# Row sums from VectorE's output step, squared distances on ScalarE, and the choice of experts spread over VectorE's other work

## The reference

```python
x = x + attention(layernorm(x))     # linear attention with running sums over the tokens
x = x + experts(layernorm(x))       # 8 experts, each token goes to the one with the largest logit
x = x + time_mix(layernorm(x))
x = x + experts(layernorm(x))

def layernorm(x, eps=1e-5):
    m = mean(x); v = var(x)         # over the 128 values of a token
    return (x - m) / sqrt(v + eps)
```

## Time and profile before

| what | value |
|---|---|
| median of three runs | 301.19 us |
| the profiled execution | 301.99 us, of which the span that the trace covers is 300.3 us |
| PE, DVE, ACT, POOL busy in the span | 93%, 79%, 61%, 75% |
| attention, from the first `project_qk` to the last tile of it scattered in time for the experts' first stage | about 9 to 73 us |
| experts, first time | about 78 to 156 us |
| time mix | about 157 to 230 us |
| experts, second time | about 230 to 300 us |

### The profile page before, as it was taken

One profiled execution on the slowest core, in us unless ns is written; L12 is line 12 of the kernel. 1 busy time (PEld: TensorE's weight loads), 2 busy tenths in 40 slices (PEclk: granted clock), 3 DMA queues, 4 the chain that ended last, 5 costly groups with the idle time before them and its releaser, 6 DMA issues.

```text
span 300.3 us, 7709 instructions
## 1 busy us (share of the span) xinstructions
PE 278.1 (93%) x2179; PEld 242.9 (81%) x2179; DVE 238.6 (79%) x1018; ACT 183.3 (61%) x543; POOL 225.7 (75%) x296
## 2 busy tenths in 40 slices
PE   7989999986899999999999899999799799999994
PEld 7556676764599999999984688877599799999994
DVE  4888999999787887777753999888977499777773
ACT  2876666532489876666630774652399566666661
POOL 3868388887878888887562757888578888888654
PEclk9999999999999999999999999999999799999998
DMA  6898810001332554321105400111321455332100
GB/s 183 244 353 222 89 40 29 27 29 33 96 75 80 127 110 112 90 74 61 33 5 170 113 0 1 45 48 45 75 81 48 116 120 111 102 95 58 46 25 2
DMA packets 32521, 25.64 MB, mean 85 GB/s; under 512 B 6000, under 2 KB 28785, under 8 KB 32480
## 3 DMA queue, kind: packets, MB, share of 16 engines
q1 hardware_dynamic: 27328, 16.51, 23.2%
q0 software_dynamic: 4576, 8.54, 8.7%
q10 hardware_dynamic: 576, 0.10, 0.2%
HBM read 14.57 MB, written 11.53 MB: 87 GB/s over the span
## 4 chain that ended last, share of the span: by engine, by line
PE 52%; DVE 16%; POOL 16%; issue 7%; DMA 6%; SPq 1%; ACT 0%; DVEq 0%; POOLq 0%; ACTq 0%
PE pair L1648 20%; PE pair L1634 14%; POOL sorted L511 10%; PE bank L1634 5%; POOL rows L485 3%; DVE stats L826 3%; PE bank L1624 2%; DMA sorted<-rows,place 2%; DVE zT L1066 2%; DMA rows<-x_mid 1%; DMA xs<-sorted 1%; DVE mv L831 1%; PE pair L1473 1%; DVE qk L1059 1%; PE pair L1419 1%
## 5 line engine op out<-in xcount | busy, mean ns | idle before, releaser
L1648 PE MATMUL pair<-w2s,hT 128*128 x624 | 83.6, 278 | 0.6 <-issue 0.4
L511 POOL DMA_INDIRECT sorted<-rows,place x64 | 64.7, 1010 | 17.8 <-issue 15.3
L1648 PEld LDWEIGHTS pair<-w2s,hT 128*128 128x128 f32 x624 | 76.5, 194 | 1.0 <-issue 0.7
L1634 PE MATMUL pair<-xsT,w1s 128*128 128x128 f32 x432 | 60.3, 277 | 0.9 <-ACT xsT L765 0.9
L1634 PEld LDWEIGHTS pair<-xsT,w1s 128*128 128x128 f32 x432 | 54.4, 194 | 1.7 <-DVE tm L1134 1.0
L688 ACT COPY w1s<-w1all 128x516 f32 x78 | 49.4, 635 | 3.6 <-DVE etab L1208 2.5
L531 POOL DMA_INDIRECT out<-ys,xs x39 | 39.4, 1009 | 12.7 <-DVE ys L1280 7.3
L531 POOL DMA_INDIRECT x_mid<-ys,xs x39 | 39.4, 1010 | 12.4 <-DVE ys L1280 7.2
L765 ACT COPY xsT<-bank 128x128 f32<-128x128 f32 x78 | 20.8, 267 | 43.5 <-PE bank L1624 41.6
L1280 DVE SCALAR_TENSOR_TENSOR ys<-pair,xs 128x128 f32<-128x128 f32 x78 | 27.2, 349 | 24.4 <-PE pair L1648 24.3
L1270 DVE TENSOR_SCALAR hT<-pair,w1s 128x128 f32<-128x128 f32 x112 | 34.4, 346 | 1.3
(11 more groups left out here) (172 smaller groups left out, 522.5 us busy)
## 6 DMA issues: line engine op xcount, KB each, us to landing
xs<-sorted SPq DMA_DIRECT2D x78, 66.0 KB, 1.8
w1all<-in_L_ffn_W_b SPq DMA_DIRECT2D x8, 258.0 KB, 6.0
rows<-in_L_attn_a_x SPq DMA_DIRECT2D x8, 256.0 KB, 4.0
w2s<-in_L_ffn_W SPq DMA_DIRECT2D x8, 256.0 KB, 6.0
rows<-x_mid SPq DMA_DIRECT2D x8, 256.0 KB, 4.9
sorted<-pad SPq DMA_DIRECT2D x30, 66.0 KB, 3.3
sorted<-rows,place POOLq DMA_INDIRECT x64, 2.4
x_mid<-ys,xs POOLq DMA_INDIRECT x39, 2.3
```

The costliest lines, as they stand in the source:

```text
L511: pool.indirect_dma_start(sorted_rows[l], bass.IndirectOffsetOnAxis(ap=place[:, t:t + 1], axis=0), rows[:, t, :], None).then_inc(s_sent[l] ...
L1634: mm = nc.tensor.matmul(bank[2 + 2 * half + i % 2][:, c * P:(c + 1) * P], w1s[i % NW][:, f:f + P], xsT[i % NB][:], start=True, stop=True)
L1648: mm = nc.tensor.matmul(bank[6 + i % 2][:, 0:P], hT[i % NB][:, c], w2s[:, bass.ds(e, 1), c, :].rearrange("p o d -> p (o d)"), start=(c == ...
```

## The change

1. Statistics. `new_rows` also writes the sum of each new row (`accum_out`, into `rsum`). `row_means(g)` turns four sums into means, one small instruction. ScalarE's new `squares(g)` computes, per tile, the square of (mean - x) and writes its sum over the row into `vsum`; `row_veps` makes variance plus eps of it. For attention's rows `bn_stats` and `bn_aggr` are gone, in the slots and for group 7 at the head of the experts. The other place where they are used (time mix) stays as it was.
2. ScalarE's order. `squares(k-2)` and `row_veps(k-2)` stand ahead of the normalized rows; these are cut into two halves with `evac_o(k-1)` between.
3. VectorE's order. In slots from 3 on, the first four steps of the choice of group `k-3` stand among the sums, reciprocals and rows of group `k-2`; the other four among `mask_scores`, `row_means`, `phi` and `add_state`, which now follows `phi`. `scan_z` stands ahead of `placed`.
4. GpSimd's order. In slots 4 to 8 one tile fewer is scattered ahead of `row_scales`, and one more behind it.

```diff
 SENDS_OF_ATTENTION = [(range(a, b), range(b, c)) for a, b, c in
-                      ((0, 0, 0), (0, 0, 0), (0, 0, 0), (0, 0, 1), (1, 4, 4), (4, 7, 7), (7, 10, 10), (10, 13, 14),
-                       (14, 17, 20), (20, 26, 28))]
+                      ((0, 0, 0), (0, 0, 0), (0, 0, 0), (0, 0, 1), (1, 3, 4), (4, 6, 7), (7, 9, 10), (10, 12, 14),
+                       (14, 16, 20), (20, 26, 28))]
...
+            def squares(g):
+                act.wait_ge(AS["mean"], g + 1)
+                for t in range(g * GT, (g + 1) * GT):
+                    last = nc.scalar.activation(unread_rows[:, t % GT], val(t), ACT.Square, bias=rows[:, t, MEAN:MEAN + 1],
+                                                scale=-1.0, accum_out=vsum[:, t:t + 1])
+                last.then_inc(AS["sq"], 1)
+
             def row_veps(S, b):
...
+                if S is AS:
+                    act.wait_ge(AS["sq"], b + 1)
+                    nc.scalar.activation(veps2[:, t], vsum[:, t], ACT.Copy, bias=EPS, scale=1.0 / D
+                                         ).then_inc(AS["ve2"], 1)
+                    return
...
-                if k + 2 < NG:
-                    norm(AS, k + 2)
                 if k == NG:
                     evac_o(k - 1)
                 if k - 2 >= 0:
+                    squares(k - 2)
                     row_veps(AS, k - 2)
+                if k + 2 < NG:
+                    norm(AS, k + 2, 0)
                 if 0 <= k - 1 < LASTG:
                     evac_o(k - 1)
+                if k + 2 < NG:
+                    norm(AS, k + 2, 1)
...
                     if i == l:
+                        if l == 0:
+                            squares(LASTG)
                         row_veps((AS, BS)[l], LASTB)
...
-                                                     op0=ALU.mult, op1=ALU.add)
+                                                     op0=ALU.mult, op1=ALU.add,
+                                                     accum_out=rsum[:, g * GT + j:g * GT + j + 1])
...
+            def row_means(g):
+                dve.wait_ge(AS["xnew"], g + 1)
+                nc.vector.tensor_scalar(column(MEAN, tiles(g)), rsum[:, tiles(g)], 1.0 / D, None, ALU.mult
+                                        ).then_inc(AS["mean"], 1)
...
+            def add_attention_and_choose(g, b):
+                bounded_sums(g)
+                sum_logits(b)
+                reciprocals(g)
+                scale_logits(0, AS, b)
+                new_logits(g)
+                bias_logits(0, AS, b)
+                new_rows(g, 0)
+                new_rows(g, 1)
+                max_logit(0, b)
+                new_rows(g, 2)
+                new_rows(g, 3)
...
-                if 0 <= k - 2:
-                    add_attention(k - 2)
+                if k == 2:
+                    add_attention(0)
+                if k >= 3:
+                    add_attention_and_choose(k - 2, k - 3)
                 if 0 <= k - 1:
                     mask_scores(k - 1)
...
-                if k == 2:
-                    dve.wait_ge(AS["xnew"], k - 1)
-                    moments(AS, 2, k - 2)
-                if k == 1 or k == 2:
-                    add_state(k - 1)
-                if k - 3 >= 0:
-                    measure_choose_and_add_state(k - 3, k - 2)
+                if k >= 3:
+                    lead_logits(0, AS, k - 3)
+                if k >= 2:
+                    row_means(k - 2)
+                if k >= 3:
+                    rank_leaders(0, AS, k - 3)
+                if k < NG:
+                    phi(k)
+                if k >= 3:
+                    top_rank(0, k - 3)
+                if 1 <= k < NG:
+                    add_state(k - 1)
+                if k >= 3:
+                    one_hot(0, AS, k - 3)
                 if k == NG:
                     placed(0, AS, k - 3)
                     return
-                phi(k)
+                scan_z(k)
                 if k - 3 >= 0:
                     placed(0, AS, k - 3)
-                scan_z(k)
...
-                        dve.wait_ge(S["xnew"], NG)
-                        moments(S, 2, LASTG)
+                        row_means(LASTG)
                         placed(l, S, LASTB - 1)
```

More of the change, by code:

```diff
@@ L172, in hybrid_block @@
         stats2 = sb("stats2", [P, NT, 6])
+        rsum = sb("rsum", [P, NT])
+        vsum = sb("vsum", [P, NT])
+        unread_rows = sb("unread_rows", [P, GT, D])
         mv1 = sb("mv1", [P, NT, 2])
@@ L259, in hybrid_block @@
         AS = {n: sem(f"a_{n}") for n in BOTH + ("qkp vp rel v phi z zq kvT kv scores am upd state o oe y "
-                                                "dmax rden lold lnew").split()}
+                                                "dmax rden lold lnew mean sq").split()}
         BS = {n: sem(f"b_{n}") for n in BOTH + "ve1 ve1p scan mix sig vm x2T x2Te logits lnew".split()}
@@ L609, in fetch_table, with norm @@
                 nc.scalar.activation(unread[:], neg_half[:], function)
-            def norm(S, g):
+            def norm(S, g, half=None):
                 p = g % 2
@@ L616, in norm @@
                 after(act, S["xT"], g - 1)
-                for j in range(GT // 2 if g == 0 else GT):
+                for j in range(GT // 2 if half == 1 else 0, GT // 2 if g == 0 or half == 0 else GT):
                     t = g * GT + j
@@ L625, in norm @@
                                                     scale=rstd1[:, t:t + 1])
-                last.then_inc(S["xn"], 1)
+                if half != 0:
+                    last.then_inc(S["xn"], 1)
             def evac_xT(S, g, read):
@@ L1011, in choose_and_measure @@
                 row_moments(BS, g, 3)
[L1013 to L1026, removed]
-                dve.wait_ge(AS["st2"], 2 * g + 1)
-                row_moments(AS, g, 0)
-                rank_leaders(0, AS, b)
-                row_moments(AS, g, 1)
-                top_rank(0, b)
-                row_moments(AS, g, 2)
-                one_hot(0, AS, b)
-                row_moments(AS, g, 3)
             def mask_scores(g):
```

## The result

The changed kernel takes 311.76 us (median of 6 runs, 310.18 to 312.33), the kernel before 301.1 us in the same comparison (6 runs). The ratio is 1.0331, 95% interval 1.0291 to 1.0371: slower by 10.7 us. The forecast was 303.1 in a range of 300.0 to 306.0; the time lies outside it.

The account below looks back on a forecast made before the run. The prediction took PE's chain to bound the kernel, through tile 15's DMA and the experts' matmuls. Tile 15 at +1.2 and the experts' head at +0.7 made +1.9 us on the median 301.19: 303.1, range 300.0 to 306.0.

Parts of the forecast that it names:

- PE sets the slot: Attention slots: PE's chain sets their 7.30 us, so VectorE's gain of about 0.4 us a slot buys nothing.
- ScalarE's loop: Slots 2 to 5: 7.5 + 4r us each, r = 0.13 for reading a square's sum; 2.2 us later in all.
- the rule: A VectorE instruction with two SBUF inputs and a GpSimd instruction reading SBUF exclude each other while the first runs.
- second rival: Slots 4 to 7: POOL's product (T + 2.3, T: project_qk's start) blocks the choice; about +1.5, 304.6; chance 0.32 with dearer read.
- the prediction's own sign of this rival: In the choice of experts, `scale_logits` or `bias_logits` taking over 1 us would show the second rival.
- at most a few tenths in slots 6 and 7: VectorE's masked scores come 0.8 us later, filling its former slack before PE's updates, at this cost.
- one swap of tables: ScalarE: Square needing another table set would swap twice in seven slots, 18 us and more, near 320; chance 0.02.
- VectorE's accumulation: Row sums on VectorE: 0.1 us for each of four accumulations, 0.4 a slot.
- The power: POOL's power takes 1.04 to 1.3 us instead of 1.96, the scan having moved away, and waits for `veps` every slot.
- Tile 15: POOL's scatter of tile 15 into the sorted array goes at 73.4 us, 1.2 later than 72.22.
- the squares at the head: Head of the experts: ScalarE's four squares for the last group delay PE's chain by 0.2 + 4r = 0.7 us.
- the rival with 0.32: The second rival's block in the slots, or a dearer read of ScalarE's sums: 304.2 to 307 us, chance 0.32.

Follow-up runs that it names:

- choose_behind: Changed kernel with the first four steps of the choice of experts put back behind the masked scores; 309.94 us, ratio 1.0236.
- no_squares: both_undone with one small ScalarE instruction writing a constant in place of a group's four squares; 303.31 us, ratio 1.0063.
- both_undone: Changed kernel with slot 1's state added ahead of phi and the choice's first four steps behind the masked scores; 306.67 us, ratio 1.0134.
- product_behind_scatter: Changed kernel with GpSimd's product issued behind each attention slot's first sorted scatter instead of ahead of it; 308.71 us, ratio 1.0228.
- order_before_no_squares: statistics_alone with one small ScalarE instruction writing a constant in place of a group's four squares; 300.2 us, ratio 0.9945.
- fill_for_clock: both_undone with two unused matmuls added in TensorE's waits, in slots 7 and 8; 305.17 to 306.75 us.
- statistics_alone: Kernel before, all orders and scatter table kept, with row sums from VectorE's output step and squares on ScalarE; 306.69 us, ratio 1.0149.

## Why the prediction was wrong, point by point

The step that failed is the one that took VectorE off the path: "PE sets the slot, VectorE's state add waits for PE's updates in any order". On it the sum had no term for GpSimd's product holding VectorE up. The runs show that term in two places, slot 1 (1.54 us of waiting) and the choice of experts in slots 4 to 6 (4 us of slots), together 2.0 of the 3.3% by the ratios below. What the sum did price, ScalarE's loop, came as foretold (point 4), so the mechanism was right as far as it went; over half of the loss is what had no term.

1. **Slot 1 wasn't in it.** The change puts `phi` ahead of the state in every slot; the prediction read in the earlier trace rows that `phi` stands behind GpSimd's product in just that slot, quoted the rule for it, and never asked what stands behind `phi` after the change. After it, TensorE stood 2.05 us behind its updates until the state was there. That is 1.54 us in the trace, 3.3 by medians. All rows for it were on record.
2. **The choice of experts: right mechanism, wrong case, wrong price.** The second rival put the product at T + 2.3 and the sums at T + 2.2 to 2.6. With T = 58.29 - 1.14 = 57.15, the product came at T + 2.4 and the first sum at T + 2.0. The row that stood was one ahead of the two named, `sum_logits`, in slots 5 and 6, and `scale_logits` in slot 4, the prediction's own sign of this rival. A coincidence computed to a few tenths was given less than a third of the chance. Its price failed as well: 0.3 to 0.5 us a slot took it that the mask would be late by a part of the product. The step stood for the whole of it: 1.15 to 1.51 us of waiting for the mask in each slot. The slots grew by 0.8, 0.7 and 2.5 us over those of `choose_behind`, 1.3 of the last through the clock: 4 us in slots 4 to 6, where about 1.5 stood for the whole rival.
3. **VectorE has no slack.** The working said that the later rows and mask cost "at most a few tenths in slots 6 and 7", since TensorE's updates set the slot. `no_squares` shows slots of 7.8 us by the new order alone, with a wait of 0.86 us for the state in slot 4, and in slot 6, behind one more hold by the product, 0.46 for the mask and 0.97 for the state. Behind the squares most of this is hidden.
4. **ScalarE's loop was right.** 7.5 + 4r with r = 0.13, 8.0 us; `both_undone` has 8.08 in slots 3 to 5, with no wait of ScalarE there but 1.29 for the turned keys, and the changed kernel 8.24 and 8.08 in slots 2 and 3. The read costs about 0.1 (0.40 a square against 0.29 a normalization). The forecast of one swap of tables at 0.02 held: the trace has one load.
5. **VectorE's accumulation was overpriced.** A row takes 0.27 from start to start with its 0.08 us read beside it, against 0.26 before: 0.01, not 0.1.
6. **The power did not come free.** It was to take 1.04 to 1.3; it took 2.00 at the end of slot 5 and 1.89 in slot 7, with VectorE's scan beside it both times (56.14 to 57.42, 74.23 to 75.51). That it would wait for ScalarE's variance in each slot was foretold (1.6 to 5.9 us).
7. **Tile 15 and the head.** 73.4 was said, 81.83 came, 75.46 with points 1 and 2 undone. For the squares at the head 0.7 was said; the runs leave 0 to 2 as their price.

By the ratios: 3.3% in all; about 1.0 is the choice of experts (1.0331 to 1.0236), 1.0 slot 1 (to 1.0134), 0.1 the table (to 1.012), 0.3 the head (to 1.0092), and 0.9 ScalarE's loop with VectorE's new order. The ratios have intervals of 0.4 to 0.7 to each side, so the first two steps are about as large as their own uncertainty, and the others smaller. The first stands by `product_behind_scatter` as well (1.0228), the second by the waits in the trace; the split of the rest is not shown.

Of the chance: the rival with 0.32 was the right place to look, and its range, 304.2 to 307, was still too low. Nor did the block simply follow from the rows and the rule that the one that comes first goes first: the steps that stood in slots 4 to 6 have rows that begin 0.58, 0.10 and 0.37 us ahead of the product's.

## What to carry to other kernels

Where two engines exclude each other, list every instruction that the change moves, with its start against the other engine's long instruction, and price a hit at the whole of that instruction plus what is queued behind it, on the engine that waits. A start a few tenths ahead of the long instruction is a hit too. Here work taken from an engine that isn't the bound bought nothing that the runs can show (`order_before_no_squares`, with the variance left out), while the squares cost 2% and the two collisions of the new order 1% each. A loop that becomes the longest hides the next one behind it; undo both before calling one of them harmless.

## What was not expected of the hardware

- ScalarE's accumulator is read by an instruction of its own: 32 of them, 197 ns each by the groups of the page, about 0.1 us a square on its queue. VectorE's read takes 81 ns and overlaps the next row.

```profile
L646 ACT ACTIVATION_READ_ACCUMULATOR unread_rows<-rows 128x1 f32 x32 | 6.3, 197 | 0.0
L989 DVE DVE_READ_ACCUMULATOR rows<-pair,rden,rows 128x1 f32 x32 | 2.6, 81 | 0.0
```

- A held instruction shows no idle time: its row begins where it could have gone, and its duration grows (0.18 to 1.72). In slot 1 `phi` began 0.84 us ahead of the product's own row, beside the issue of another transfer by GpSimd, and in slot 6 the sum 0.37 ahead. The hold begins while GpSimd still issues the transfer right ahead of the product. Over all traces but that of `fill_for_clock`, fifteen VectorE instructions with two SBUF inputs began 0.42 us or more into such an issue, and all stood until the product was over; five began 0.10 to 0.29 into it and took 0.18 to 0.21. Beside issues that something else followed, the small steps of choice and places took 0.25 or less, however far in they began (146 cases from 0.42 on, up to 75 us). Why the product holds them before its own row begins isn't shown.
- TensorE's granted clock falls to 0.50 for some microseconds, in most of these traces once or twice in the middle of the run, and small edits move the place: 65 to 69 and 246 to 250 us in the changed kernel, 70 to 77 and 223 to 227 in `both_undone`, 79 to 82 and 222 to 226 in `statistics_alone`, 237 to 240 in the kernel before, nowhere in `order_before_no_squares`. What lies behind the experts' first pass takes 144.11 to 144.32 us in the six traces with a fall between 237 and 250 us, and 142.35 to 142.73 in the seven with none there but at the very end, so such a fall costs about 1.7 us. In the two with a fall at 222 to 227 it takes 143.15 and 142.77. Runs of the kernel before at a mean clock of 1.000 took 300.2 to 300.5 us, at 0.994 300.5 to 302.8, at 0.983 303.4 to 304.1. So 3 us of a difference between two single runs can be clock.
